# SyncE's order in an attention and expert kernel: where the load of the inverse sums and the load of the transposed activations stand in the queue

## The chip, the cores and the metric

The kernel runs on one core of one Trainium2 chip. The metric is the device time of one execution in microseconds (us), the median of several. The engines are TensorE (PE; its weight loads are shown as PEld), VectorE (DVE), ScalarE (ACT), GpSimd (POOL) and SyncE (SP), which issues nearly all DMAs here. Each engine works through its own instructions strictly in the order of the program, and waits at semaphores.

## The reference, cut to what matters

The input has 8 samples of 512 tokens and 256 channels. Each is normalised (layernorm without weights); then

```python
x = x + attention(xn) + ffn(xn)
# attention: 16 heads of 16 channels; q, k, v and the output each go through a low-rank product
resonance = einsum('bli,hi->blh', x, basis)          # 32 harmonics
q         = einsum('blh,oh->blo', resonance, amp * cos(phase))
out       = softmax(q k^T / 4) v                     # per head, 512 x 512
# ffn: 8 experts (2 per token, weights from a softmax) of width 352, and a shared expert of width 704
```

Before attention the rows of q and k, the low-rank rows and the sums of the softmax are sent through DRAM, since they have to change their place among the partitions.

## The kernel before, in words

**Stages.** The first 366 us or so hold the normalisation, the routing and the routed experts. From about 373 us on the kernel runs the attention of the 8 samples, with the shared expert of each sample woven in between. Only this second stage is touched.

**Slots and steps.** The second stage is a row of slots, called through `slots` on each engine: `slot(b, g)` for sample `b` of 8 and head group `g` of 4 (four heads), after two lead-in slots `(-1, 2)` and `(-1, 3)`. A slot has 8 steps `t`. In each step PE computes one transposed score tile (`score_T`, L1426) into the one PSUM pair `st_pair`, and ACT turns it into exponentials (`exponent`, L1065); `score_T` of step `t` waits for the exponential of step `t - 1`. In the same step PE computes plain scores of the following group (`score`, L1353), of which DVE takes maxima (`maximum`, L1874). The exponentials times the values are PE's L1438. Between these stand pieces of the shared expert (L1402, L1415, L1515), and the small products of the low-rank paths.

**The maxima.** At step 4 PE turns the maxima of the next group (`turn_max`, L1368), at step 5 ACT copies them to `top_T` (`max_rows`, L1024), SyncE sends them to `q_rows` (`load_max`, L632), and the first `score_T` of the next slot waits for that to land.

**The inverse sums.** The sums of the softmax of two groups are gathered into `o_inv` (`move_sums`, L639), and the values into `ao` (`move_values`, L647). In an even slot, step 5, DVE inverts the sums (`invert_sum`, L1924); SyncE stores them to DRAM (`store_inverse`, L652), and in the following odd slot loads them back spread over 128 rows (`load_inverse`, L658) into `o_sum`. It first waits for the store to land. POOL multiplies (`normalise`, L787), and ACT copies the product (`ao_high`, L1077). In ACT's program `ao_high` stands at step 4 of the odd slots, behind that step's exponential, ahead of `max_rows` and of the exponential of step 5. In POOL's program, `hidden` and `hidden_low` of the shared expert and `ao_low` follow `normalise`.

**The low-rank rows.** In slot `(b, 3)`, step 2, PE computes the low-rank product of sample `b + 2` (`low_rank`, L1452) from the transposed activations, which SyncE has loaded (`load_xT`, L588, 1 MB). ACT and DVE split it (L1057 in step 2, L1905 in step 3), and SyncE stores both parts (`store_low_rank`, L607 and L609). In slot `(b, 1)` the like happens for rows of q: PE projects at step 2, ACT splits in step 2 (L1018), DVE in step 3 (L1867), and SyncE stores both parts (`store_qk`, L625 twice and L627).

**SyncE's order before.** An odd slot begins with `load_inverse`, in group 3 followed by `load_x_b` (L597, the residual of the sample, 512 KB), then come the stores of the low-rank rows or of q, then `load_max` and `load_rows` (L551, four loads of 192 KB). In group 2 `load_xT(b + 2)` comes behind `load_rows`. The two buffers of transposed activations, `xT_bs`, are used in turn by `for_rows` (low-rank product) and `for_shared` (shared expert): that of `for_rows(b + 2)` is that of `for_shared(b - 1)`, whose last use lies in slot `(b - 1, 3)`.

The lines on which ACT's order rests are these:

```python
if now:
    exponent(b, g, t)
...
if t == 4 and g % 2 and moved(ppb, ppg // 2):
    ao_high(ppb, ppg // 2)     # waits for p_nm, which normalise on POOL raises
```

Of the kernel before, what the change touches and what calls it, by code (L numbers as in the profile page):

```python
# [33 lines left out]
class Steps:  # L34
# [13 lines left out]
    def wait(self, n=None):  # L48

        self.eng.wait_ge(self.sem, self.value(n))  # L50
# [13 lines left out]
def build_program(nc, x, attn, gate_w, w_gate, w_up, w_down, sw_gate, sw_up, sw_down, out):  # L64
# [45 lines left out]
    def sem(name):  # L110
        return ctx.enter_context(nc.semaphore(name))

    with ctx:
# [218 lines left out]
        b_r, b_v, b_qk, b_s, b_mt, b_st, b_pv, b_gu, b_ha, b_res, b_dn, b_po = (  # L332
            sem(f"b_{n}") for n in ("r", "v", "qk", "s", "mt", "st", "pv", "gu", "ha", "res", "dn", "po"))
# [49 lines left out]
        def for_rows(b):  # L383

            return xT_bs[(b + 1) % 2 if b > 1 else 1]
# [15 lines left out]
        def of(b):  # L401

            return NB - 1 - b

        def there(b):

            return 0 <= b < NB

        def after(b, g, n):

            return (b + (g + n) // NG, (g + n) % NG)
# [14 lines left out]
        def moved(b, p):  # L426

            return there(b) and (b, p) != (LAST, 1)
# [27 lines left out]
        def _(sp):  # L456
# [84 lines left out]
            def load_rows(b, g):  # L541
                for i in range(2):
                    wait(sp, qk_st[i], (b * 2 + g // 2 + 1) * 48)
                if b == 0:
                    sp.wait_ge(minus_st, 16)
                else:
                    wait(sp, b_st, (b - 1) * 32 + g * 8 + 8)
                for which, rows in ((1, k_rows[g]), (0, q_rows[g])):
                    n = 50 if b == 0 and which else 48
                    for i in range(2):  # L550
                        sp.dma_start(rows[64 * i:64 * i + n, :, :].bitcast(F32),  # L551
                                     qk_dram[b % 2, which].rearrange("(j i) r l -> i r j l", i=2)[i][0:n, 2 * g:2 * g + 2, :]).then_inc(qk_in[g], 16)
# [28 lines left out]
            def load_xT(b):  # L581
                if b == 1:
                    for i in range(4):
                        sp.wait_ge(c_st[i], 16 * ((NS + 3 - i) // 4))
                if b == 2:
                    wait(sp, b_r, 2)
                wait(sp, b_gu, (b - 2) * SFT)
                sp.dma_start(for_rows(b)[:, :, :, :].rearrange("p a k l -> p (a k l)").bitcast(F32), xT_dram[of(b)]).then_inc(xT_in, 16)  # L588

            def load_xF(b):  # L590
                wait(sp, b_r, min(b + 2, NB))
                wait(sp, b_gu, (b - 1) * SFT)
                sp.dma_start(for_shared(b)[:, :, :, :].rearrange("p a k l -> p (a k l)").bitcast(F32), xT_dram[of(b)]).then_inc(xF_in, 16)

            def load_x_b(b):
                wait(sp, o_st, b * 32)
                sp.dma_start(o_b[:, :, :], x[of(b)].rearrange("(t p) d -> p t d", p=P)).then_inc(ob_in, 16)  # L597

            def store_out(b, h):
                wait(sp, d_po, b * 2 + h + 1)  # L600
                sp.dma_start(out[of(b), h * 2 * P:(h + 1) * 2 * P, :].rearrange("(t p) d -> p t d", p=P),
                             o_b[:, 2 * h:2 * h + 2, :]).then_inc(o_st, 16)

            def store_low_rank(b):
                wait(sp, r_in, b * 48)
                wait(sp, a_r, b + 1)
                sp.dma_start(r_dram[HI].rearrange("h n l -> n h l"), r_hi[:, :].bitcast(F32)).then_inc(r_st, 16)  # L607
                wait(sp, d_r, b + 1)
                sp.dma_start(r_dram[LO].rearrange("h n l -> n h l"), r_lo[:, :].bitcast(F32)).then_inc(r_st, 16)  # L609

            def load_low_rank(b):
                wait(sp, r_st, (b + 1) * 32)
                wait(sp, b_qk, (b - 1) * 4)
                wait(sp, b_v, (b - 1) * 2)
                for c, part in enumerate((HI, HI, LO)):
                    sp.dma_start(r_rows[b % 2][c * HARM:(c + 1) * HARM, :, :].bitcast(F32), r_dram[part]).then_inc(r_in, 16)

            def store_qk(b, n):
                which, half, i = n % 2, n // 2, n % 2
                if b >= 2:  # L620
                    wait(sp, qk_in[NG - 1], (b - 1) * 64)
                dst = qk_dram[b % 2, which, 8 * half:8 * half + 8, 0:48].rearrange("h (c r) l -> h c r l", c=3)
                wait(sp, a_qk, b * 4 + n + 1)
                for c in ((0, 1), (0, 2))[which]:
                    sp.dma_start(dst[:, c, :, :], qk_hi[i][:, :].bitcast(F32)).then_inc(qk_st[i], 16)  # L625
                wait(sp, d_qk, b * 4 + n + 1)
                sp.dma_start(dst[:, (2, 1)[which], :, :], qk_lo[i][:, :].bitcast(F32)).then_inc(qk_st[i], 16)  # L627

            def load_max(b, g):
                wait(sp, a_mt, b * NG + g + 1)  # L630
                for par in range(2):
                    sp.dma_start(q_rows[g][64 * par + 48:64 * par + 50, :, :].rearrange("a j (t q) -> a j t q", q=P).bitcast(F32),  # L632
                                 top_T[g % 2][16 * par:16 * par + 16, :].bitcast(F32)).then_inc(m_in[g % 2], 16)

            def move_sums(b, g):
                p, h = 2 * b + g // 2, g % 2
                wait(sp, inv_st, p * 16)
                wait(sp, a_ot, b * NG + g + 1)
                sp.dma_start(o_inv[64 * h:64 * h + 64, :], o_T[h][16:128:32, :]).then_inc(sum_in[h], 16)  # L639

            def move_values(b, g):
                p, h = 2 * b + g // 2, g % 2
                wait(sp, p_ao, p)
                wait(sp, a_ot, b * NG + g + 1)
                for j in range(4):
                    o = 64 * h + 16 * j
                    sp.dma_start(ao[o:o + 16, :], o_T[h][32 * j:32 * j + 16, :]).then_inc(ao_in[h], 16)  # L647

            def store_inverse(b, p):
                wait(sp, inv_in, (2 * b + p) * 16)  # L650
                wait(sp, d_inv, 2 * b + p + 1)
                sp.dma_start(inv_dram[p], o_inv[:, :]).then_inc(inv_st, 16)  # L652

            def load_inverse(b, p):
                wait(sp, inv_st, (2 * b + p + 1) * 16)
                wait(sp, p_nm, 2 * b + p)
                heads = inv_dram[p].rearrange("(h o r) l -> h o (r l)", h=8, o=1).to_broadcast([8, 16, L])
                sp.dma_start(o_sum[:, :], heads).then_inc(inv_in, 16)  # L658

            def slot(b, g):  # L660
                (pb, pg), (ppb, ppg), (nb, ng), (rb, rg) = after(b, g, -1), after(b, g, -2), after(b, g, 1), after(b, g, 3)
                if ppg % 2 and moved(ppb, ppg // 2):
                    load_inverse(ppb, ppg // 2)
                if g == 3 and there(b):
                    load_x_b(b)
                if pg % 2 and moved(pb, pg // 2):
                    move_sums(pb, pg)
                    move_values(pb, pg)
                if g == 0 and there(b + 1):
                    store_qk(b + 1, 0)  # L670
                if g == 1 and there(b + 1):
                    store_qk(b + 1, 2)
                if g == 2 and there(b - 1):
                    store_out(b - 1, 0)
                if g == 3 and there(b + 2):
                    store_low_rank(b + 2)
                if there(nb):
                    load_max(nb, ng)
                if there(rb):
                    load_rows(rb, rg)  # L680
                if g == 2 and there(b + 2):
                    load_xT(b + 2)
                if g == 3 and there(b + 2):
                    load_low_rank(b + 2)
                if g == 3 and there(b) and there(b + 1):
                    load_xF(b + 1)
                if pg % 2 == 0 and moved(pb, pg // 2):
                    move_sums(pb, pg)
                    move_values(pb, pg)
                if pg % 2 and moved(pb, pg // 2):  # L690
                    store_inverse(pb, pg // 2)
                if g == 0 and there(b + 1):
                    store_qk(b + 1, 1)
                if g == 1 and there(b + 1):
                    store_qk(b + 1, 3)
                if g == 2 and there(b - 1):
                    store_out(b - 1, 1)

# [1321 lines left out]
```

## Time and profile before

| | |
|---|---|
| median of 3 runs | 979.91 us (979.81 to 980.3) |
| the profiled execution: own time | 981.48 us |
| the profiled execution: span in the profile | 979.7 us |
| PE busy | 878.4 us (90%) |
| DVE busy | 611.4 us (62%) |
| ACT busy | 582.2 us (59%) |
| POOL busy | 400.7 us (41%) |
| mean granted clock of PE | 0.949 of full speed |
| mean DMA traffic | 150 GB/s |

PE is busy for nine tenths of the span, but in the second stage it is tied to the others step by step. The profile's "busy" leaves waiting out; the waits stand in views of their own. In the timeline a row gives the start, the time taken, the engine, the line, the tiles, the shape and the count of instructions merged into it, and in brackets the idle time before it and what ended it. Rows of SPq are issues of DMAs: their time is that of issuing, and not that of the transfer.

### The profile page before, as it was taken

The numbers are of one execution on the slowest core, as the hardware profiler recorded it, in microseconds if no ns is written. First come the engines' busy times: TensorE is split into PE (matmuls) and PEld (weight loads), VectorE is DVE, ScalarE is ACT, GpSimd is POOL, SyncE is SP. The second block draws the span as 40 slices with busy tenths as digits, with TensorE's granted clock in tenths as the row PEclk, the third lists the DMA queues.
The fourth block names the chain that finished last, engine by engine and source line by source line (L and its number), as shares of the span: only waits on it lengthen the run. The fifth ranks groups of instructions, "written<-read, shape, count | busy, mean of one in ns | idle before, by whom it ended". The sixth has DMA issues, their size and how long they took to land.

```text
span 979.7 us, 19365 instructions
## 1 busy us (share of the span) xinstructions
PE 878.4 (90%) x6423; PEld 608.5 (62%) x6424; DVE 611.4 (62%) x923; ACT 582.2 (59%) x932; POOL 400.7 (41%) x384
## 2 busy tenths in 40 slices
PE   4745999999999985788999998999998999999998
PEld 3425999999999982244644644645644645645546
DVE  7777844434434446576786686786786686787642
ACT  5745744444444441477677577677677577677673
POOL 2002622222222203247357356356366356366463
PEclk9865999999999995699999999999999999999999
DMA  9983756222222314356656656667566567564220
GB/s 308 388 249 118 240 143 176 67 75 75 64 75 69 71 57 135 115 132 169 199 144 199 184 149 190 186 155 211 168 154 201 159 154 213 166 161 121 73 83 22
DMA packets 90951, 147.35 MB, mean 150 GB/s; under 512 B 17433, under 2 KB 51745, under 8 KB 88065
## 3 DMA queue, kind: packets, MB, share of 16 engines
q1 hardware_dynamic: 84192, 128.58, 44.5%
q0 software_dynamic: 6480, 17.70, 6.5%
q8 instruction: 43, 0.70, 0.3%
q10 hardware_dynamic: 208, 0.14, 0.1%
q14 instruction: 28, 0.22, 0.1%
HBM read 86.58 MB, written 54.71 MB: 144 GB/s over the span
## 4 chain that ended last, share of the span: by engine, by line
PE 61%; DMA 15%; DVE 14%; SPq 4%; issue 3%; ACT 2%; POOL 1%; ACTq 0%; POOLq 0%; DVEq 0%
PE bank L1438 8%; PE bank L1294 8%; PE s_pair L1276 7%; PE st_pair L1276 7%; DVE top L1874 7%; PE s_pair L1353 6%; PE bank L1402 5%; PE bank L1515 5%; DMA xT_b<-xn_T_split 5%; DMA q_rows<-top_T 4%; PE st_pair L1426 4%; PE bank L1284 2%; PE bank L1259 2%; DMA low_rank_rows<-ro 2%; SPq L632 1%
## 5 line engine op out<-in xcount | busy, mean ns | idle before, releaser
L1874 DVE TENSOR_REDUCE top<-s_pair 128x2 f32<-128x1024 f32 x252 | 308.7, 1225 | 159.9 <-PE s_pair L1353 159.4
L1065 ACT ACTIVATE prob<-st_pair 128x1024 f32<-128x1024 f32 x256 | 262.7, 1026 | 119.1 <-PE st_pair L1426 118.0
L750 POOL DMA_INDIRECT xg<-xn_rows,token_of x71 | 78.9, 1111 | 224.6 <-PE bank L1259 168.9
L1402 PE MATMUL bank<-xT_b,w_sh 64*128 64x512 f32 x960 | 142.5, 401 | 1.0 <-DVE ro L1943 0.2
L1353 PE MATMUL s_pair<-k_rows,q_rows 48*128 48x512 f32 x504 | 121.7, 477 | 20.3 <-DVE top L1874 19.1
L1438 PE MATMUL bank<-prob,v_ones 128*32 128x512 f32 x1024 | 126.4, 612 | 0.0
L1426 PE MATMUL st_pair<-q_rows,k_rows 50*128 50x512 f32 x512 | 110.2, 425 | 17.4 <-DMA q_rows<-top_T 12.9
L796 POOL DMA_INDIRECT y_b<-expert_rows,slot_of x64 | 63.0, 984 | 148.5 <-PE st_pair L1426 141.8
L1402 PEld LDWEIGHTS bank<-xT_b,w_sh 64*128 64x128 f32 x960 | 91.2, 185 | 30.5 <-issue 7.6
L1353 PEld LDWEIGHTS s_pair<-k_rows,q_rows 48*128 48x128 f32 x504 | 49.3, 190 | 77.0 <-DVE top L1874 65.0
L1294 PE MATMUL bank<-w_exp,c_hT 128*128 (+1 forms) x639 | 94.2, 292 | 1.0 <-ACT c_y L985 1.0
L1294 PEld LDWEIGHTS bank<-w_exp,c_hT 128*128 128x128 f32 (+1 forms) x639 | 81.1, 190 | 1.4 <-issue 1.4
L771 POOL TENSOR_TENSOR h_f<-h_f,u_half 128x512 f32<-128x512 f32 x40 | 51.6, 1290 | 72.9 <-DVE h_f L1889 72.9
L1276 PE MATMUL s_pair<-w_exp,xg_T 128*128 x432 | 80.3, 335 | 0.0
L1276 PE MATMUL st_pair<-w_exp,xg_T 128*128 x420 | 76.5, 330 | 0.0
L1426 PEld LDWEIGHTS st_pair<-q_rows,k_rows 50*128 50x128 f32 x512 | 49.7, 189 | 42.4 <-DMA q_rows<-top_T 16.4
L1515 PEld LDWEIGHTS bank<-w_sh,h_T 64*128 64x128 f32 x952 | 66.0, 186 | 8.1 <-issue 2.9
L1276 PEld LDWEIGHTS s_pair<-w_exp,xg_T 128*128 128x128 f32 x432 | 70.5, 192 | 0.3
L1515 PE MATMUL bank<-w_sh,h_T 64*128 64x256 f32 x952 | 70.0, 282 | 0.1
L980 ACT ACTIVATE c_hT<-bank 128x384 fp32r<-128x384 f32 x71 | 34.9, 491 | 55.6 <-PE bank L1284 55.6
L1276 PEld LDWEIGHTS st_pair<-w_exp,xg_T 128*128 128x128 f32 x420 | 66.9, 188 | 0.0
L1438 PEld LDWEIGHTS bank<-prob,v_ones 128*32 128x32 f32 x1024 | 27.1, 110 | 60.2 <-issue 56.6
(234 smaller groups left out, 1201.5 us busy)
## 6 DMA issues: line engine op xcount, KB each, us to landing
xT_b<-xn_T_split SPq DMA_DIRECT2D x14, 1024.0 KB, 7.5
qk_rows<-qk_hi SPq DMA_DIRECT2D x56, 256.0 KB
q_rows<-qk_rows SPq DMA_DIRECT2D x64, 192.0 KB
k_rows<-qk_rows SPq DMA_DIRECT2D x56, 192.0 KB
expert_rows<-c_y SPq DMA_DIRECT2D x71, 128.0 KB, 1.7
xn_T_split<-x_T SPq DMA_DIRECT2D x8, 1024.0 KB, 6.4
qk_rows<-qk_lo SPq DMA_DIRECT2D x28, 256.0 KB
x_all<-in_L_attn_x_dram SPq DMA_DIRECT2D x8, 512.0 KB, 8.3
```

The lines of the kernel that those rows point to most:

```text
L750: pool.indirect_dma_start(xg[s % 4][:, :], None, xn_dram, bass.IndirectOffsetOnAxis(token_of[:, s:s + 1], 0)).then_inc(c_x[s % 4], 16)
L771: pool.tensor_tensor(h, h, u_half[:, :], ALU.mult).then_inc(p_hf, 1)
L796: pool.indirect_dma_start(y_b[:, t, k, :], None, y_dram, bass.IndirectOffsetOnAxis(slot_of[:, k, of(b) * TPB + t:of(b) * TPB + t + 1], 0)) ...
L1065: act.activation(prob[n % 3][:, 2 * jp:2 * jp + 2, :].rearrange("p j l -> p (j l)"), st_pair[:, :], ACT.Exp, scale=HD ** -0.5).then_inc(a_ ...
L1276: ins = pe.matmul(gu_bank[i % 2][n][:, 0:F], xg_T[i % 2][:, a * KT + k, :], w, start=(m == 0 and k == 0), stop=(m == 2 and k == KT - 1))
L1294: ins = pe.matmul(y_bank[:, 0:D], c_hT[i % 2][0:n, a, k, :], w, start=(m == 0 and k == 0), stop=(m == 2 and k == FT - 1))
L1353: ins = pe.matmul(score_pair(b, g, v)[:, i * 512:(i + 1) * 512], q_rows[g][r:r + 48, jp, qt * P:(qt + 1) * P], k_rows[g][r:r + 48, jp, :], ...
L1402: ins = pe.matmul((g_bank, u_bank)[up][:, :], w_sh[rows, a, o:o + P], for_shared(b)[rows, c, k, :], start=(n == 0 and i == 0), stop=(n == ...
L1426: ins = pe.matmul(st_pair[:, i * 512:(i + 1) * 512], k_rows[g][r:r + QK_ROWS, jp, kt * P:(kt + 1) * P], q_rows[g][r:r + QK_ROWS, jp, :], s ...
L1438: ins = pe.matmul(ot_bank[32 * j:32 * j + 32, :], v_ones[:, kt, 4 * g + j, :], prob[(b * 16 + g * 4 + kt) % 3][:, j, :], start=(kt == 0), ...
L1515: ins = pe.matmul((g_bank, u_bank)[to][:, 0:D], h_T[rows, a, f, t * P:(t + 1) * P], w_sh[rows, c, S_GU + f * D:S_GU + (f + 1) * D], start= ...
L1874: dve.tensor_reduce(top[g % 2][:, :, jp, qt], score_pair(b, g, v)[:, :].rearrange("p (i k) -> p i k", i=2), AX_X, ALU.max).then_inc(d_max, 1)
```

## The change

Three things are moved in SyncE's program. `load_inverse` and `load_x_b` go behind `store_qk(b + 1, 0 or 2)`, `store_out` and `store_low_rank`, directly ahead of `load_max`. `load_xT(b + 2)` goes from the middle of slot `(b, 2)` to the end of slot `(b, 1)`, except for the one in the lead-in slot `(-1, 2)`, which stays. `load_xT(b)` waits in addition until the low-rank products of all samples ahead of `b` are done (`b_r >= b`).

```diff
@@ load_xT(b)
                 wait(sp, b_gu, (b - 2) * SFT)
+                wait(sp, b_r, b)
                 sp.dma_start(for_rows(b)[...], xT_dram[of(b)]).then_inc(xT_in, 16)
@@ slot(b, g)
-                if ppg % 2 and moved(ppb, ppg // 2):
-                    load_inverse(ppb, ppg // 2)
-                if g == 3 and there(b):
-                    load_x_b(b)
                 if pg % 2 and moved(pb, pg // 2):
                     move_sums(pb, pg)
                     move_values(pb, pg)
...
                 if g == 3 and there(b + 2):
                     store_low_rank(b + 2)
+                if ppg % 2 and moved(ppb, ppg // 2):
+                    load_inverse(ppb, ppg // 2)
+                if g == 3 and there(b):
+                    load_x_b(b)
                 if there(nb):
                     load_max(nb, ng)
                 if there(rb):
                     load_rows(rb, rg)
-                if g == 2 and there(b + 2):
+                if (b, g) == (-1, 2):
                     load_xT(b + 2)
...
                 if g == 1 and there(b + 1):
                     store_qk(b + 1, 3)
+                if g == 1 and there(b + 2):
+                    load_xT(b + 2)
```

## Rows read from the trace of the kernel before

**Rows 1.** The page, chain that ended last, shares by line.

```profile
PE bank L1438 8%; PE bank L1294 8%; PE s_pair L1276 7%; PE st_pair L1276 7%; DVE top L1874 7%; PE s_pair L1353 6%; PE bank L1402 5%; PE bank L1515 5%; DMA xT_b<-xn_T_split 5%; DMA q_rows<-top_T 4%; PE st_pair L1426 4%; PE bank L1284 2%; PE bank L1259 2%; DMA low_rank_rows<-ro 2%; SPq L632 1%
```

**Rows 2.** Waits of PE and PEld from 440 us on: total, times, longest.

```profile
PE st_pair L1426 <- DMA q_rows<-top_T: 10.6, 8, 2.2
...
PE bank L1452 <- DMA xT_b<-xn_T_split: 3.1, 4, 1.4
...
PEld bank L1452 <- DMA xT_b<-xn_T_split: 6.0, 6, 1.8
```

**Rows 3.** Timeline of SyncE in and ahead of a slot of group 3.

```profile
514.93 0.43 SPq L588 DMA_DIRECT2D xT_b<-xn_T_split  x1
...
522.80 0.65 SPq L658 DMA_DIRECT2D o_sum<-inverse_rows  x1
523.49 0.46 SPq L597 DMA_DIRECT2D o_b<-in_L_attn_x_dram  x1
...
527.09 0.70 SPq L609 DMA_DIRECT2D low_rank_rows<-ro  x1
```

**Rows 4.** Timeline of POOL, ACT and PE in the same slot.

```profile
526.92 1.28 POOL L787 TENSOR_TENSOR ao<-ao,o_sum 128x512 f32<-128x512 f32 x1 [1.30 <-DMA o_sum<-inverse_rows]
...
528.24 0.63 ACT L1077 ACTIVATE ao_T<-ao 128x512 fp32r<-128x512 f32 x1
...
528.98 0.27 ACT L1024 ACTIVATE top_T<-bank 32x128 fp32r<-32x128 f32 x1
...
531.04 0.40 PE L1426 MATMUL st_pair<-q_rows,k_rows 50*128 50x512 f32 x2
...
533.10 1.33 PE L1402 MATMUL bank<-xT_b,w_sh 64*128 64x512 f32 x10
535.57 0.50 PE L1426 MATMUL st_pair<-q_rows,k_rows 50*128 50x512 f32 x2 [1.13 <-DMA q_rows<-top_T]
```

**Rows 5.** Timeline of SyncE, POOL, ACT and PE in a slot of group 1.

```profile
558.34 0.63 SPq L658 DMA_DIRECT2D o_sum<-inverse_rows  x1
...
564.17 0.56 SPq L627 DMA_DIRECT2D qk_rows<-qk_lo  x1
...
563.93 1.29 POOL L787 TENSOR_TENSOR ao<-ao,o_sum 128x512 f32<-128x512 f32 x1 [2.35 <-DMA o_sum<-inverse_rows]
...
565.25 0.63 ACT L1077 ACTIVATE ao_T<-ao 128x512 fp32r<-128x512 f32 x1
...
566.73 1.03 ACT L1065 ACTIVATE prob<-st_pair 128x1024 f32<-128x1024 f32 x1 [0.41 <-PE st_pair L1426]
...
568.54 0.40 PE L1426 MATMUL st_pair<-q_rows,k_rows 50*128 50x512 f32 x2
...
570.03 0.50 PE L1353 MATMUL s_pair<-k_rows,q_rows 48*128 48x512 f32 x2 [0.66 <-DVE top L1874]
```

**Rows 6.** Timeline of the last slot of group 1 that stores rows of q.

```profile
854.80 0.57 SPq L627 DMA_DIRECT2D qk_rows<-qk_lo  x1
...
854.84 0.64 ACT L1077 ACTIVATE ao_T<-ao 128x512 fp32r<-128x512 f32 x1
```

**Rows 7.** Timeline around group 1's end: sums sent, then inverted; POOL's addition.

```profile
575.71 1.26 SPq L639 DMA_DIRECT2D o_inv<-o_T  x1
...
585.24 0.34 DVE L1924 RECIPROCAL o_inv<-o_inv 128x32 f32<-128x32 f32 x1
...
532.60 2.39 POOL L809 TENSOR_TENSOR o_b<-o_b,y_b 128x1024 f32<-128x1024 f32 x1
```

**Rows 8.** Windows: busy time by engine, granted clock of PE, DMA share, GB/s.

```profile
440.00:979.00 539.00, 510.40 (x4080) 293.40 (x4076) 371.83 (x445) 366.55 (x491) 288.05 (x263) 1.00 0.56 157
54.00:58.00 4.00, 0.61 (x2) 0.13 (x2) 3.77 (x8) 2.02 (x1) 0.00 (x0) 0.54 0.51 105
522.00:524.00 2.00, 1.65 (x8) 0.89 (x6) 0.92 (x1) 1.01 (x1) 2.00 (x3) 1.00 0.10 29
```

**Rows 9.** Timeline of PE, the longest idle time ahead of the routing.

```profile
55.53 0.40 PE L1239 MATMUL s_pair<-hot_b,from_here 128*128 128x256 bf16 x1 [4.87 <-DVE hot_b L1764]
```

## The prediction

> **What bounds the kernel now.** I read the chain of waits first [rows 1]: in the attention stage the end is set by PE's own work with short pieces of DVE between, and by DMAs that come late: the transposed activations (5% of the span) and the maxima (4%). That share counts the whole flight of a DMA. What PE really loses stands in the list of waits [rows 2]: 10.6 us in 8 waits for the maxima at the head of a slot, and for the transposed activations 3.1 us on PE and 6.0 us on its weight loads, over six samples. The two overlap, so the move of that load can give 6.0 us at most. In this stage PE is busy for 510.40 of 539.00 us at a granted clock of 1.00 [rows 8]; it has no reserve that could take in a new wait.
>
> Then I read the timeline of SyncE beside those of POOL and ACT, since the change moves the load of the inverse sums, and somebody waits for it. In the slot of group 3 the load is issued at 522.80 [rows 3], `normalise` starts at 526.92 having waited 1.30 us for it, and `ao_high` starts at 528.24, at once behind it [rows 4]. In the slot of group 1 the times are 558.34, 563.93 (after a wait of 2.35 us) and 565.25 [rows 5]. So in both kinds of slot POOL already waits for this load, and ACT takes the product as soon as it is there. What the reader is to see: this load has no slack left. Behind `ao_high` on ACT stand `top_T` and the exponential of step 5, for which PE's `score_T` of step 6 waits.
>
> **Part 1: the load goes behind the stores.** SyncE waits in order. The store of the second low-rank part is issued when DVE has made it, in step 3: at 527.09, for 0.70 us [rows 3]. The load now follows at 527.8 instead of 522.80, 5.0 us later. In group 1 it follows the store of q at 564.17 plus 0.56, so at 564.75 instead of 558.34, 6.4 us later [rows 5]. Both new issues come at about the time at which its product was used (528.24 and 565.25).
>
> How long the load takes: 4.12 us from issue to POOL's start in the one case, 5.59 in the other [rows 3 to 5]. The 4.12 were with a drained queue (29 GB/s in 522 to 524 us [rows 8]). Now the stores stand just ahead of it, small in group 3 (192 KB each), 256 KB three times in group 1. I take 4.2 and 4.6 us, nearer to the drained case, since one store at most is still under way; 4.1 and 5.6 are the bounds.
>
> Group 3: 527.8 + 4.2 = 532.0; `normalise` 1.28; `ao_high` starts at 533.3, 5.1 us later than before. Then `ao_high` 0.63, `top_T` 0.27, the exponential 1.03 [rows 4, 5]: 535.2, where `score_T` of step 6 was at 531.04. With a tenth or so of overlap PE loses 4.1 us in one idle stretch. It does not end there: the first `score_T` of the next slot waits for the maxima, 6.6 us from `top_T` at 528.98 to 535.57, of which 1.13 us were idle [rows 4]. `top_T` is 5.1 us later, so by that rule the next slot starts 5.1 us later. If the maxima land faster, PE's own work decides: 4.1 less the 1.13 that are no longer waited, 3.0 us. I take 4.8, nearer to the upper end, because nothing else in that flight changes. Only where sample `b + 2` exists has the load a store ahead of it: `b` from 0 to 5, six slots, 6 x 4.8 = 29 us.
>
> Group 1: 564.75 + 4.6 + 1.29 + 0.63 + 0.27 + 1.03 = 572.6, less 0.2 of overlap 572.4, against 568.54: 3.9 us. Of these 0.66 are taken in, since PE waited that long for a maximum right behind [rows 5], which DVE now makes meanwhile: 3.2 us. These slots exist for `b` from 1 to 6. In four of the six the store of q ends not 0.5 us ahead of the old `ao_high` but behind it, as in the last (855.37 against 854.84 [rows 6]); part of that lateness ACT already had, so I count 0.7 us more: 2 x 3.2 + 4 x 3.9 = 22 us.
>
> Queued behind the delayed instructions: on POOL `hidden`, `ao_low` and `hidden_low`, three of them, the first of which ACT's copy of the shared expert's rows needs after the exponential of step 5. They run while ACT works off `top_T` and the exponential, so they add nothing. On SyncE `load_max` stands behind the load, but it has to wait for `top_T` anyway, and that comes well after the issue.
>
> **Part 2: the residual's load moved with it.** 512 KB, also issued some 5 us later in group 3. POOL's addition of it starts at 532.60 [rows 7], but POOL itself is now 5 us late, and `normalise` and three more stand ahead of it. Nothing, as long as part 1 holds; without that cover one or two us a sample.
>
> **Part 3: the transposed activations a group ahead.** Issued at the end of group 1's slot, about 575.7 where it stands [rows 7], instead of behind `load_rows` in the next one (the like of 514.93, used at 522.47 [rows 3]). It has most of a slot more to land. That saves between 3.1 and 6.0 us in all [rows 2]; I take 4. The low-rank rows get no longer behind 512 KB of residual, perhaps another 1 us. What the 1 MB is now ahead of: the sums' second move (575.71) and the four moves of values. DVE inverts at 585.24 [rows 7], 9.5 us later; with the 7.5 us that the 1 MB needed from 514.93 to 522.47 that just fits, so 0, at most 1 us a sample. The new wait for `b_r` is for products finished over a slot earlier: 0.
>
> **Part 4: PE's clock.** Each of the twelve slots gets one idle stretch of 3 to 5 us. The longest in this stage was 2.2 us [rows 2], with a clock of 1.00 throughout; in the first stage an idle time of 4.87 us [rows 9] was followed by a clock of 0.54 over 54 to 58 us [rows 8], which mixes the 1.2 and the 2.4 GHz levels. The new stretches lie between. None falling would be 0; all falling for 4 us each, with half of that lost, 24 us. I take 5, nearer to the 2.2 us that changed nothing, as most stretches lie below 4.87.
>
> **Sum.** 29 + 22 - 4 - 1 + 5 = 51 us. The profiled execution (981.48 us, its span 979.7) would become 1032.5; that run is 1.6 us above the median of 979.91, on which I put the same sum: 1031 us. Low bound: even slots 3.0, odd ones 2.7 and 3.4, savings 7, no clock: 18 + 19 - 7 = 30, 1010. High: the loads at 5.6 us, 6 x 6.2 + 22 + 6, savings 3, clock 18: 80, 1060.
>
> **Where a page and the rows differ.** In a drained queue this 256 KB load took 4.12 us until POOL ran. The Trainium skill, page DMA: Bandwidth & Descriptors, section on the anatomy of one DMA, puts a DMA at about 2.0 us fixed plus its bytes at 436 GB/s, an estimate of 2.6 us here (it was fitted on GpSimd's path). With that the sum would be 24 us lower, 1007; the trace does not agree in any of the slots read.
>
> **Rivals.**
>
> A. The load is faster than before, because what slowed it was the traffic of 1 MB and of the row loads, now elsewhere. If it took 2.5 us, the twelve slots would each lose some 1.7 to 2 us less: about 1009. The 4.12 us in the drained queue speak against it [rows 3, 4, 8]. 12%.
>
> B. The clock falls in nearly every stretch. Price 20 us or more above part 4: 1050 to 1065. For it: the fall around the 4.87 us; against: none at 2.2. The skill's page TensorE: Matmul & The Clock Gate, section on the clock gate, says that PE drops to its half rate when it idles long enough and comes back by sustained work, which would speak for B. 10%.
>
> C. Faster: the moved load of the activations removes the wait ahead of the low-rank product, up to 6.0 us, and the stores of the low-rank rows, no longer behind 768 KB, make the low-rank rows early, while ACT is not held: 973. The point from which it decides is the time between the store's end and the product's use. It needs `normalise` done by 528.6 in group 3, that is within 0.8 us of the load's issue, when it alone takes 1.28. Nearly excluded: 2%.
>
> D. The order changes nothing, since SyncE stood at the load until the inverse had been stored, and reached the stores late already: 976 to 981. But 4.3 us lie between the load's issue and that of the last store in group 3 (522.80 and 527.09), 5.8 us in group 1. 2%.
>
> My forecast, 1010 to 1050, keeps 74%. About 0.2% is what a measurement of this kernel can tell from no change. Slower by more than that takes in A, B and the forecast: 0.96; faster 0.02, same 0.02. The range 1005 to 1056 leaves out part of A and of B.
>
> **What would show it.** In the profile after: a new wait of ACT at L1077 for POOL L787 of 3 to 5 us, some twelve times; POOL's wait at L787 for the inverse sums grown from 1.3 to 2.4 us to 6 or more; a new wait of PE at L1426 for ACT's exponential, about 45 us in twelve; the wait at L1452 gone; windows with a clock under 1.00 in the attention stage if part 4 is real. I am wrong if the load is issued after the stores and POOL still starts within 2 us of the old time, or if PE's waits for the exponential stay near nothing.

## The result, and the profile after

The changed kernel takes 1080.22 us (median of 4, 1078.17 to 1085.28) against 980.11 us before (four runs; the 979.91 us above are the median of the first three): a ratio of 1.1000, 95% interval 1.0959 to 1.1041. It is slower by 100 us. The direction is the one forecast, the size is twice the forecast 51 us, and outside the range.

The profiled execution has a span of 1083.5 us (its own time is 1085.28 us, the slowest of the four), so the traces differ by 103.8 us, a little more than the medians (979.7 us before). Lines of the code behind the change stand one to three further down: L658 is now L659, L609 is L610, L787 is L790, L1077 is L1080, L1426 is L1429.

First the page of the changed kernel: busy time, the granted clock in 40 slices, and the chain that ended last.

```profile
PE 914.3 (84%) x6423; PEld 630.5 (58%) x6424; DVE 608.5 (56%) x923; ACT 579.9 (54%) x932; POOL 401.8 (37%) x384
...
PEclk9955999999999757989989888898898988989999
...
DMA o_sum<-inverse_rows 9%; PE bank L1441 8%; PE bank L1405 8%; PE bank L1297 7%; PE s_pair L1356 7%; PE st_pair L1429 6%; PE s_pair L1279 6%; PE st_pair L1279 6%; PE bank L1518 6%; DVE top L1877 4%; PE bank L1287 2%; PE bank L1551 2%; PE bank L1262 2%; ACT prob L1068 2%; POOL ao L790 1%
```

Against [rows 1] the activations and the maxima have gone from the leading shares of the chain, and the load of the inverse sums, which did not stand in it, leads it with 9%. PE's busy time went up from 878.4 to 914.3 us although it runs the same products: 35.9 of the 103.8 us are products that took longer, the other 67.9 us are idle time. From the middle on the clock's digits are 8 about as often as 9, where they were 9 throughout in the kernel before. In the stage from 440 us on, PE's granted clock is 0.90 on average and its products take 545.99 us, against 1.00 and 510.40 us [rows 8].

The list of waits of the changed kernel from 440 us on (total, times, longest) shows the chain of who waited for whom, POOL for the load, ACT for POOL, PE for ACT, and what has gone from PE:

```profile
POOL ao L790 <- DMA o_sum<-inverse_rows: 125.9, 12, 11.1
...
ACT ao_T L1080 <- POOL ao L790: 106.4, 13, 10.3
...
PE st_pair L1429 <- ACT prob L1068: 89.2, 13, 9.1
...
PE s_pair L1356 <- DVE top L1877: 2.1, 5, 1.1
```

Twelve waits of PE for ACT, as predicted, but of 5.6 to 9.1 us and not of some 4 (the thirteenth is 0.4 us). The waits of [rows 2] for the maxima and the activations do not occur any more, and PE's waits for DVE fell from 7.9 to 2.1 us: the long idle stretches took them in.

The timeline of the changed kernel in a slot of group 3, the counterpart of [rows 3, 4], in the order of the chain:

```profile
546.03 0.70 SPq L610 DMA_DIRECT2D low_rank_rows<-ro  x1
546.84 0.65 SPq L659 DMA_DIRECT2D o_sum<-inverse_rows  x1
547.55 0.45 SPq L598 DMA_DIRECT2D o_b<-in_L_attn_x_dram  x1
...
556.16 1.26 POOL L790 TENSOR_TENSOR ao<-ao,o_sum 128x512 f32<-128x512 f32 x1 [11.14 <-DMA o_sum<-inverse_rows]
...
557.45 0.63 ACT L1080 ACTIVATE ao_T<-ao 128x512 fp32r<-128x512 f32 x1 [10.28 <-POOL ao L790]
...
558.14 1.00 ACT L1068 ACTIVATE prob<-st_pair 128x1024 f32<-128x1024 f32 x1
...
559.19 0.80 PE L1429 MATMUL st_pair<-q_rows,k_rows 50*128 50x512 f32 x2 [9.06 <-ACT prob L1068]
```

Every link is where the prediction had it. One number differs: from the issue of the load at 546.84 to POOL's start at 556.16 pass 9.32 us, and 4.2 had been taken. Read in the same way, all six slots of group 3 have 9.1 to 9.3 us. The last row also shows the clock: two products of `score_T` take 0.80 us together where they took 0.40 to 0.50 [rows 4].

In group 1, the counterpart of [rows 5]:

```profile
591.98 0.57 SPq L628 DMA_DIRECT2D qk_rows<-qk_lo  x1
592.65 0.63 SPq L659 DMA_DIRECT2D o_sum<-inverse_rows  x1
...
599.62 1.26 POOL L790 TENSOR_TENSOR ao<-ao,o_sum 128x512 f32<-128x512 f32 x1 [10.24 <-DMA o_sum<-inverse_rows]
...
602.65 0.80 PE L1429 MATMUL st_pair<-q_rows,k_rows 50*128 50x512 f32 x2 [6.15 <-ACT prob L1068]
```

Here the load took 6.97 us (6.4 to 7.0 over the six slots), against the 4.6 taken. In the six slots of group 1 of the kernel before, read in the same way, it had taken 5.4 to 7.4 us already.

What went on in the DMA queue while POOL waited stands in the windows of the changed kernel (length, busy time of PE, PEld, DVE, ACT, POOL, granted clock, DMA share, GB/s):

```profile
546.00:548.00 2.00, 2.00 (x19) 0.55 (x13) 1.73 (x3) 1.17 (x2) 0.00 (x0) 1.00 0.18 47
548.00:550.00 2.00, 2.00 (x16) 1.24 (x14) 1.23 (x1) 0.00 (x0) 0.00 (x0) 1.00 0.69 201
550.00:552.00 2.00, 0.13 (x2) 0.00 (x0) 1.23 (x1) 0.00 (x0) 0.00 (x0) 1.00 0.69 209
552.00:554.00 2.00, 0.00 (x0) 0.00 (x0) 0.00 (x0) 0.00 (x0) 0.00 (x0) 1.00 0.18 63
554.00:556.00 2.00, 0.00 (x0) 0.00 (x0) 0.00 (x0) 0.00 (x0) 0.00 (x0) 0.53 0.12 45
```

In the first window the stores of the low-rank rows are in flight, in the fourth what is left after the bulk of both loads. Both times the 16 engines are busy at 0.18: three of sixteen are 0.19. The trace also records each packet, the pieces in which a DMA moves its bytes, and these say the same: from 546.0 to 547.5 us 3.0 packets are under way at a time, never more than 4, and from 552 to 554 us 3.1, never more than 5. The load had to wait, in a queue that was nearly empty by GB/s, and that is the thing the experiments had to explain. The fifth window shows the second surprise: PE's clock falls in the middle of the wait and is half when work comes back.

### The profile page after: what moved, and what is told of

Read it like the earlier page. It is cut to its first block, busy times and chain, and to the rows that moved or that the text cites. A ratio compares the mean times of both kernels' runs of the same rounds, so it can differ in the third digit from the quotient of the medians.

```text
span 1083.5 us, 19371 instructions
## 1 busy us (share of the span) xinstructions
PE 914.3 (84%) x6423; PEld 630.5 (58%) x6424; DVE 608.5 (56%) x923; ACT 579.9 (54%) x932; POOL 401.8 (37%) x384
## 4 chain that ended last, share of the span: by engine, by line
PE 68%; DMA 12%; DVE 9%; ACT 4%; issue 3%; SPq 2%; POOL 2%; ACTq 0%; POOLq 0%; DVEq 0%
DMA o_sum<-inverse_rows 9%; PE bank L1441 8%; PE bank L1405 8%; PE bank L1297 7%; PE s_pair L1356 7%; PE st_pair L1429 6%; PE s_pair L1279 6%; PE st_pair L1279 6%; PE bank L1518 6%; DVE top L1877 4%; PE bank L1287 2%; PE bank L1551 2%; PE bank L1262 2%; ACT prob L1068 2%; POOL ao L790 1%
## 5 line engine op out<-in xcount | busy, mean ns | idle before, releaser
L1429 PE MATMUL st_pair<-q_rows,k_rows 50*128 50x512 f32 x512 | 120.4, 465 | 95.7 <-ACT prob L1068 92.9
L753 POOL DMA_INDIRECT xg<-xn_rows,token_of x71 | 81.1, 1142 | 222.4 <-PE bank L1262 167.3
L1405 PE MATMUL bank<-xT_b,w_sh 64*128 64x512 f32 x960 | 151.0, 421 | 1.0 <-DVE ro L1946 0.4
L1356 PE MATMUL s_pair<-k_rows,q_rows 48*128 48x512 f32 x504 | 126.0, 494 | 14.0 <-DVE top L1877 12.7
L1441 PE MATMUL bank<-prob,v_ones 128*32 128x512 f32 x1024 | 130.0, 627 | 0.0
L1429 PEld LDWEIGHTS st_pair<-q_rows,k_rows 50*128 50x128 f32 x512 | 53.8, 205 | 125.5 <-ACT prob L1068 107.7
L1405 PEld LDWEIGHTS bank<-xT_b,w_sh 64*128 64x128 f32 x960 | 96.9, 198 | 31.8 <-issue 6.8
L1356 PEld LDWEIGHTS s_pair<-k_rows,q_rows 48*128 48x128 f32 x504 | 52.2, 202 | 71.5 <-DVE top L1877 53.8
L1080 ACT ACTIVATE ao_T<-ao 128x512 fp32r<-128x512 f32 x15 | 9.5, 631 | 106.4 <-POOL ao L790 106.4
L790 POOL TENSOR_TENSOR ao<-ao,o_sum 128x512 f32<-128x512 f32 x15 | 19.0, 1267 | 126.0 <-DMA o_sum<-inverse_rows 125.9
```

The lines of the kernel that those rows point to most:

```text
L753: pool.indirect_dma_start(xg[s % 4][:, :], None, xn_dram, bass.IndirectOffsetOnAxis(token_of[:, s:s + 1], 0)).then_inc(c_x[s % 4], 16)
L1356: ins = pe.matmul(score_pair(b, g, v)[:, i * 512:(i + 1) * 512], q_rows[g][r:r + 48, jp, qt * P:(qt + 1) * P], k_rows[g][r:r + 48, jp, :], ...
L1405: ins = pe.matmul((g_bank, u_bank)[up][:, :], w_sh[rows, a, o:o + P], for_shared(b)[rows, c, k, :], start=(n == 0 and i == 0), stop=(n == ...
L1429: ins = pe.matmul(st_pair[:, i * 512:(i + 1) * 512], k_rows[g][r:r + QK_ROWS, jp, kt * P:(kt + 1) * P], q_rows[g][r:r + QK_ROWS, jp, :], s ...
L1441: ins = pe.matmul(ot_bank[32 * j:32 * j + 32, :], v_ones[:, kt, 4 * g + j, :], prob[(b * 16 + g * 4 + kt) % 3][:, j, :], start=(kt == 0), ...
```

## The experiments

**Theory 1** after the result: the loss comes from the load of the inverse sums alone. It is late twice, since it is issued late and then stands in the DMA queue behind stores; the idle time that follows costs PE its clock too. **Rivals**: the activations' load has a share; the residual's 512 KB stretch the flight; the flight is long at that time of the slot whatever stands ahead; the clock costs nothing. Each ratio below is against the kernel before, run on the same chip as the experiment.

**The change in its two halves.** `e1` moves only the load of the activations:

```diff
--- changed kernel
+++ e1_activations_only
@@ slot(b, g) of SyncE
+                if ppg % 2 and moved(ppb, ppg // 2):
+                    load_inverse(ppb, ppg // 2)
+                if g == 3 and there(b):
+                    load_x_b(b)
                 if pg % 2 and moved(pb, pg // 2):
...
                     store_low_rank(b + 2)
-                if ppg % 2 and moved(ppb, ppg // 2):
-                    load_inverse(ppb, ppg // 2)
-                if g == 3 and there(b):
-                    load_x_b(b)
```

> Only the load of the transposed activations moves; the loads of the inverse sums and of the residual stay where they were. Theory 1 (the loss comes from the load of the inverse sums alone): the wait ahead of the low-rank product goes, 973 to 978 us. Rival (1 MB ahead of the sums' second move delays these, and that is part of the loss): 985 us or more.

Measured: 979.0 us (10 runs) against 982.45 us of the kernel before on the same chip, ratio 0.9968 (0.9946 to 0.9990): a gain of 3 us. The time lies 1 us above what was expected. PE's wait for the activations is gone, but its wait for the maxima stays:

```profile
PE st_pair L1429 <- DMA q_rows<-top_T: 7.7, 6, 1.9
```

`e2` moves only the other two loads:

```diff
--- changed kernel
+++ e2_inverse_only
-                if (b, g) == (-1, 2):
+                if g == 2 and there(b + 2):
                     load_xT(b + 2)
...
-                if g == 1 and there(b + 2):
-                    load_xT(b + 2)
```

> Only the loads of the inverse sums and of the residual move. Theory 1: nearly all of the loss, 1080 to 1088 us, a few us more than the changed kernel, since the activations come late again. Rival (the activations' load has its share in the loss): 1060 us or less.

Measured: 1084.21 us, ratio 1.1058 (1.0996 to 1.1119). The whole loss belongs to this half. The 4 us more than the change lie within the intervals. With `e1`, which has no loss, the load of the activations is innocent.

**The two kinds of slot.** `e6` keeps the load late in group 3 alone, `e7` in group 1 alone:

```diff
--- changed kernel
+++ e6_late_in_group_3
+                if g == 1 and ppg % 2 and moved(ppb, ppg // 2):
+                    load_inverse(ppb, ppg // 2)
                 if pg % 2 and moved(pb, pg // 2):
...
-                if ppg % 2 and moved(ppb, ppg // 2):
+                if g == 3 and ppg % 2 and moved(ppb, ppg // 2):
                     load_inverse(ppb, ppg // 2)
--- changed kernel
+++ e7_late_in_group_1
+                if g == 3 and ppg % 2 and moved(ppb, ppg // 2):
+                    load_inverse(ppb, ppg // 2)
+                if g == 3 and there(b):
+                    load_x_b(b)
                 if pg % 2 and moved(pb, pg // 2):
...
-                if ppg % 2 and moved(ppb, ppg // 2):
+                if g == 1 and ppg % 2 and moved(ppb, ppg // 2):
                     load_inverse(ppb, ppg // 2)
-                if g == 3 and there(b):
-                    load_x_b(b)
```

> The changed kernel with the load of the inverse sums back at the head of the slot in group 1; it is late in group 3 alone, six slots. Theory 1 (each kind of slot pays for itself: 9.0 us of idle time and a low clock in group 3, 5.8 in group 1): some 60 of the 100 us remain, 1035 to 1045 us. Rival (the slots work on each other: a sample that is late in one group is late in the next anyway, so that most of the loss stays): 1060 us or more.

> The changed kernel with the load of the inverse sums, and that of the residual, back at the head of the slot in group 3; the first is late in group 1 alone. Theory 1 (the two groups' losses add up): 100 us less the 57 that group 3 alone kept, so 1018 to 1026 us, with a flight of 6.2 to 7 us and idle stretches of 5.5 to 6.2. Rival (they overlap): 1035 us or more.

Measured: 1036.87 us, ratio 1.0554 (1.0497 to 1.0611), and 1023.04 us, ratio 1.0467 (1.0424 to 1.0510). In parts of the time before these are 5.5% and 4.7%, together 10.2%, and the change has 10.0%. The slots pay each for itself: some 9 us for each of the six in group 3, some 7.5 us for each in group 1. The windows of the stage, of `e6` and then of `e7`, show what of this is slower products:

```profile
440.00:1037.00 597.00, 528.12 (x4083) 306.25 (x4082) 372.26 (x445) 366.20 (x492) 288.55 (x263) 0.93 0.52 140
```

```profile
440.00:1022.00 582.00, 527.36 (x4080) 301.13 (x4076) 375.58 (x445) 366.11 (x491) 287.80 (x263) 0.96 0.52 144
```

PE's products take 17.7 and 17.0 us more than the 510.40 of the kernel before, each time for six idle stretches: some 3 us a stretch.

**Late by issue, or late in the queue.** `e3` lets SyncE wait for both parts as in the change, and then issues the load first and the stores behind it. So the issue is as late as in the change, and only what stands ahead in the queue differs.

```diff
--- changed kernel
+++ e3_load_ahead_of_stores
                 if g == 1 and there(b + 1):
+                    wait(sp, a_qk, (b + 1) * 4 + 3)
+                    wait(sp, d_qk, (b + 1) * 4 + 3)
+                if g == 3 and there(b + 2):
+                    wait(sp, a_r, b + 3)
+                    wait(sp, d_r, b + 3)
+                if ppg % 2 and moved(ppb, ppg // 2):
+                    load_inverse(ppb, ppg // 2)
+                if g == 1 and there(b + 1):
                     store_qk(b + 1, 2)
...
                     store_low_rank(b + 2)
-                if ppg % 2 and moved(ppb, ppg // 2):
-                    load_inverse(ppb, ppg // 2)
```

> The changed kernel, but SyncE, having waited for both parts in step 3, issues the load of the inverse sums first and the stores behind it. The issue comes about as late as in the change. Theory 1 (the load is late twice: it is issued late, and then it stands behind the stores in the DMA queue, 9.3 us of flight in group 3 and 6.6 in group 1 against 4.1): the flight falls to 4 to 5 us, PE's idle stretches from 9.0 and 5.8 to about 4, and the time to 1020 to 1045 us. Rival (at this time of the slot the load is slow whatever stands ahead of it): flight 6 us or more, 1070 us or more.

Measured: 1053.13 us, ratio 1.0700 (1.0646 to 1.0753). The flight did what theory 1 said; the time did not come down as far. SyncE, POOL and PE of this kernel, in a slot of group 3:

```profile
544.22 0.65 SPq L659 DMA_DIRECT2D o_sum<-inverse_rows  x1
...
548.09 1.26 POOL L796 TENSOR_TENSOR ao<-ao,o_sum 128x512 f32<-128x512 f32 x1 [4.92 <-DMA o_sum<-inverse_rows]
...
551.12 0.50 PE L1435 MATMUL st_pair<-q_rows,k_rows 50*128 50x512 f32 x2 [2.83 <-ACT prob L1074]
551.46 0.39 PE L1411 MATMUL bank<-xT_b,w_sh 64*128 64x512 f32 x2
...
552.37 0.79 PE L1411 MATMUL bank<-xT_b,w_sh 64*128 64x512 f32 x2
...
558.60 0.50 PE L1435 MATMUL st_pair<-q_rows,k_rows 50*128 50x512 f32 x2 [2.54 <-DMA q_rows<-top_T]
```

The flight is 3.87 us here, 3.8 to 4.3 over all twelve slots, in both groups. The load is not slow at that time of the slot; the stores ahead of it made 2.5 and 5.2 us of its flight. PE's idle stretches at this place fell to 2.4 to 3.1 us. The time lies 8 us above the expectation, and the rows show two things that it had left out. The clock falls even after 2.83 us: the same pair of products takes 0.39 us at 551.46 and 0.79 at 552.37. It does so in all twelve slots, behind stretches of 2.40 to 3.11 us. And the maxima, sent behind the stores, now come late in the next slot (2.54 us, the last row; 13.7 us over six slots).

**The residual.** `e4` puts the 512 KB load back to the head of the slot:

```diff
--- changed kernel
+++ e4_residual_back
+                if g == 3 and there(b):
+                    load_x_b(b)
                 if pg % 2 and moved(pb, pg // 2):
...
-                if g == 3 and there(b):
-                    load_x_b(b)
```

> The changed kernel with the load of the residual (512 KB) back at the head of the slot of group 3. Theory 1 (the store ahead sets the flight): the flight in group 3 stays near 9 us, 1073 to 1085 us. Rival (the 512 KB that follow the load share its DMA engines and stretch it): the flight in group 3 falls to 5 to 6 us, PE's idle stretches there to 5, and the time to about 1050 us.

Measured: 1080.98 us, ratio 1.1002 (1.0955 to 1.1049), with a flight of 8.9 to 9.0 us in group 3. The residual is worth 0.4 us of flight and nothing in the time. That rival has fallen.

**Three engines of sixteen.** The buffer of the low-rank rows in DRAM is laid out as 32 x 3 x 512, and the store writes it through a view of 3 x 32 x 512. `e8` lays it out as 3 x 32 x 512, so that a store is 96 rows in one run, and the load takes the view instead. (Of the stage itself the second store and the load are shown; the first store, the two stores ahead of the stage and the load of the first sample's values are altered in the same way.)

```diff
--- changed kernel
+++ e8_low_rank_rows_spread
-    r_dram = nc.dram_tensor("low_rank_rows", (2, 32, 3, L), F32).ap()
+    r_dram = nc.dram_tensor("low_rank_rows", (2, 3, 32, L), F32).ap()
...
-                sp.dma_start(r_dram[LO].rearrange("h n l -> n h l"), r_lo[:, :].bitcast(F32)).then_inc(r_st, 16)
+                sp.dma_start(r_dram[LO].rearrange("n h l -> (n h) l"), r_lo[:, :].bitcast(F32)).then_inc(r_st, 16)
...
-                    sp.dma_start(r_rows[b % 2][c * HARM:(c + 1) * HARM, :, :].bitcast(F32), r_dram[part]).then_inc(r_in, 16)
+                    sp.dma_start(r_rows[b % 2][c * HARM:(c + 1) * HARM, :, :].bitcast(F32), r_dram[part].rearrange("n h l -> h n l")).then_inc(r_in, 16)
```

> The changed kernel with the buffer of the low-rank rows in DRAM laid out as the rows lie in SBUF, so that a store is one run of 96 rows and not three of 32. Theory 1 (the two stores ahead of the load use 3 of the 16 DMA engines, the share of 0.18 in the windows, and the load has to wait for just these): the share goes up, the flight in group 3 falls from 9.3 to 4 to 6 us, PE's idle stretches there from 9.0 to about 5, those of group 1 stay, and the time is 1040 to 1058 us. Rival (a store of 192 KB is slow however it is spread, since it goes to DRAM): 1073 us or more.

Measured: 1044.26 us, ratio 1.0641 (1.0581 to 1.0700), 36 us less than the change, with the same bytes in the same order of issue. (The load of these rows, which now goes through the view, comes behind all of this in the queue.) SyncE, POOL and the window behind the issue:

```profile
533.84 0.32 SPq L610 DMA_DIRECT2D low_rank_rows<-ro  x1
534.25 0.65 SPq L659 DMA_DIRECT2D o_sum<-inverse_rows  x1
...
538.46 1.26 POOL L790 TENSOR_TENSOR ao<-ao,o_sum 128x512 f32<-128x512 f32 x1 [5.63 <-DMA o_sum<-inverse_rows]
```

```profile
534.00:536.00 2.00, 2.00 (x21) 0.69 (x15) 1.53 (x2) 0.97 (x2) 0.00 (x0) 1.00 0.43 112
```

The flight in group 3 fell to 4.21 us (3.8 to 5.3 over the six), the share rose from 0.18 to 0.43, and even the issue of the store takes 0.32 us on SyncE and not 0.70. In group 1, where nothing was altered, the flight stayed at 6.2 to 7.0 us. While the second store runs (534.8 to 535.2 us) 15.6 packets are under way at a time, where the change had 3.0. So the stores ahead were slow because they used few engines. That the load shares just these engines is inferred from the packets, the share and the flight; no row names an engine. The Trainium skill, page DMA: Bandwidth & Descriptors, section "Why a DMA increments its semaphore by 16 and not by 1", gives the rule behind it: a DMA is spread over the largest number up to 16 that divides the slowest dimension (other than 1) of both sides, and those issued as here are given the lowest-numbered engines. By that rule 3 x 32 x 512 against 96 rows gives 3, and 96 rows against 96 rows gives 16; the 3.0 and 15.6 packets agree, while which engines they are no run here shows.

**The clock by itself.** `e5` gives PE products that nobody reads, ahead of `score_T` of step 6, where it would stand idle:

```diff
--- changed kernel
+++ e5_dummy_products
@@ slot(b, g) of PE
+                    if (g, t) == (1, 6) and 1 <= b < LAST:
+                        wait(pe, a_uh, lows(b, 0))
+                        for n in range(20):
+                            pe.matmul(u_bank[:, :], basis_T[...], for_shared(b)[:, HI, 0, :], start=True, stop=True)
+                    if (g, t) == (3, 6) and 0 <= b < LAST - 1:
+                        for n in range(8):
+                            pe.matmul(m_bank[64:128, :], basis_T[...].bitcast(F32), for_shared(b)[:, HI, 0, :].bitcast(F32), start=True, stop=True)
                     if now:
                         score_T(b, g, t)
```

> The changed kernel, with products whose results nobody reads put on PE ahead of score_T of step 6 in the twelve slots (20 in group 1, 8 slower ones in group 3), where PE would stand idle; nothing else is moved and the output stays the same. Theory 1 (besides the idle time itself, PE loses time because its clock falls to half in each stretch and stays there when work comes back): the clock stays at 1.00 and the time falls to 1055 to 1070 us. Rival (the clock costs nothing, the other engines set the pace after the stretch): 1076 us or more.

Measured: 1065.96 us, ratio 1.0857 (1.0798 to 1.0917). Flights and the lateness of ACT are those of the change; only PE's idle time is filled. The slot of group 3 and the windows of the whole stage, of this kernel and then of the changed one:

```profile
543.74 7.08 PE L1615 MATMUL bank<-xT_b,basis_T 128*64 128x512 f32 x16
552.86 0.50 PE L1429 MATMUL st_pair<-q_rows,k_rows 50*128 50x512 f32 x2 [2.04 <-ACT prob L1068]
```

```profile
440.00:1063.00 623.00, 591.86 (x4284) 334.67 (x4280) 367.69 (x443) 363.07 (x490) 287.35 (x262) 0.98 0.50 134
```

```profile
440.00:1083.00 643.00, 545.99 (x4101) 314.10 (x4099) 370.85 (x447) 366.07 (x494) 287.69 (x263) 0.90 0.49 131
```

The mean clock of the stage rises from 0.90 to 0.98, `score_T` behind the wait takes 0.50 us and not 0.80, and the time falls by 14 us (20 between the two profiled executions). That is a lower bound of what the clock costs, since it did not stay at 1.00 throughout, as theory 1 had it. An upper bound is what all products together take longer in the change, 35.6 us in this stage.

**Better than both.** `e9` is `e1` with the layout of `e8`, `e10` the kernel before with the layout alone:

```diff
--- kernel before
+++ e10_spread_only          (e9: the same on top of e1)
-    r_dram = nc.dram_tensor("low_rank_rows", (2, 32, 3, L), F32).ap()
+    r_dram = nc.dram_tensor("low_rank_rows", (2, 3, 32, L), F32).ap()
...
```

> The loads of the inverse sums and of the residual where they were before, the activations a group ahead, and the low-rank rows laid out as in the run before. Theory 1: the maxima sent behind the stores in group 3 land sooner, the wait of PE at the head of the next slot goes, and the time is 966 to 974 us. Rival (that flight has its length from its own small pieces): 975 to 981 us.

> The kernel before with the low-rank rows laid out as in the two runs above and nothing else: the load of the activations stays in group 2, the load of the inverse sums at the head of the slot. Theory 1 (the two gains are apart: some 3 us from the activations, the rest from the layout): 964 to 969 us, and the wait of PE for the activations is still there. Rival (each needs the other, since without the layout the activations' gain is eaten by the next wait, and the other way round): 970 us or more.

Measured: `e9` 961.91 us, ratio 0.9791 (0.9749 to 0.9833); `e10` 963.43 us, ratio 0.9839 (0.9811 to 0.9867). Both beat both kernels, and both lie below what was expected, `e9` by 4 us and `e10` by 0.6. The waits of PE from 440 us on, first of `e9`, then of `e10`:

```profile
PE s_pair L1356 <- DVE top L1877: 9.6, 24, 1.1
PE st_pair L1561 <- ACT o_T L1075: 1.0, 1, 1.0
```

```profile
PE s_pair L1353 <- DVE top L1874: 7.2, 19, 1.1
PE bank L1452 <- DMA xT_b<-xn_T_split: 2.6, 4, 1.2
```

The 10.6 us of waiting for the maxima [rows 2] are gone in both. Six of those eight waits stood at the head of a slot of group 0, for maxima that had been sent behind the low-rank stores; the other two stood at the head of a slot of group 1, and why they went too is not shown. The activations' wait stays in `e10` and goes in `e9`. The gains roughly add up, 0.3% from the activations and 1.6% from the layout against 2.1% for both, within the intervals.

## Why the prediction was wrong

**What bounds, and who waits: right.** That the load had no slack, that ACT takes its product in step 4 ahead of `top_T` and of the next exponential, that PE then stands in front of `score_T` of step 6, in twelve slots: all as forecast, link by link. `e2` shows that all of the loss is here.

**Part 1, the load's flight: the first step that failed.** It said "I take 4.2 and 4.6 us, nearer to the drained case, since one store at most is still under way". It measured 9.1 to 9.3 and 6.4 to 7.0. Nearness was judged by how much of the queue was filled, and the right question was how long the thing directly ahead takes. The trace of before had the answer: its chain of waits has the store of the second low-rank part in flight for more than 7 us, in two of the slots,

```profile
671.79 7.63 DMA low_rank_rows<-ro
...
817.52 7.48 DMA low_rank_rows<-ro
```

and its windows right behind that store have 0.19 of the DMA engines at 59 GB/s:

```profile
528.00:530.00 2.00, 2.00 (x19) 1.04 (x13) 1.37 (x3) 1.46 (x4) 1.33 (x2) 1.00 0.19 59
```

The window that the prediction read, 522 to 524 us, lies ahead of the stores and was a drained queue indeed; this one, in which the moved load would run, was three engines at work. In group 1 the 4.6 us lay below all six flights of the kernel before, 5.4 to 7.4 us, and the upper bound of 5.6 below three of them. The excess of flight is 5.1 us in six slots and some 2 in the other six, 43 us. `e3` takes it away in both groups and `e8` in group 3, in two independent ways, and they leave flights of 3.8 to 5.3 us, about what had been taken.

**The next slot's maxima.** The 4.8 us for a slot of group 3 had the rule that `top_T`'s lateness is passed on in full. In the changed kernel the next slot does not wait for the maxima at all, since SyncE sends them long after the stores are through. So the loss per slot is set by the idle stretch, 9.06 us less what it takes in, and the 6.6 us from `top_T` to the next slot was no constant: with the stores spread, in `e9` and `e10`, that wait is gone.

**Part 2, the residual at nothing: right** (`e4`, 1080.98 us). **Part 3, 4 us for the activations and 0 for what stands behind them: right in size** (`e1`, 3 us, with an interval of 1 to 5).

**Part 4, the clock: the second step that failed, a term of the right kind and too small.** Taken were 5 us; measured were 14 us at least (`e5`) and 35.6 us of longer products at most. The choice "nearer to the 2.2 us that changed nothing" was wrong: the clock fell behind all twelve stretches of 5.6 to 9.1 us, and in `e3`, where the flights were as short as the prediction had them, behind all twelve of 2.40 to 3.11. So this term would have failed with the right flights too.

**How the 51 us became 103.8 in the traces.** PE's twelve stretches come to 88.8 us, where the sum had 6 x 4.1 and 6 x 3.9 = 48; these 41 us more are about the excess of flight. But part of them was taken in: PE's idle time rose by 67.9 us in all, since its waits for the maxima, for DVE and for the activations went or shrank, and the sum had 46 for it (29 + 22 - 4 - 1). So idle time was short by 22 us, and the products, 35.9 us longer against the 5 taken, by 31. This says where PE's time went; what each cause is worth by itself is known only as `e3`, `e5` and `e8` give it, 27, 14 and 36 us, and these overlap.

**Where a page and the rows differed.** The 2.6 us from the page's fixed time and rate were no better: no flight of this load was under 3.8 us in any run. (The 24 us that this was to take off the sum do not come out of it either: 1.6 us in six slots and 2.0 in six are 22.) What did bear on it was how the transfer ahead is spread over the DMA engines. Rival A fell with the flights. B was right that the clock falls in every stretch, and its price, 20 us or more above the 5, lies between the two bounds above; the time left its range because of the flights. C and D fell.

## What to carry to other kernels

Before a transfer is put behind another in one queue, look at that other's own flight and at how many DMA engines it uses, not at the queue's GB/s: here two stores of 192 KB on three engines held the load behind them up by 5 us. The cure was a layout in DRAM that lets the store run as one block of rows, and it was worth more (16 us, `e10`) than the order of the issues (3 us, `e1`). When an engine in the middle of a lockstep takes a product at a fixed place in its program, its supply may be moved only by the slack that the trace shows, which here was none. And idle stretches of PE are to be priced with the slower products behind them, here some 3 us each.

## What the runs showed of the hardware

PE's granted clock fell from 2.4 to 1.2 GHz after shorter idle time than expected: from 440 us on never in the kernel before, whose longest idle stretch was 2.18 us, but in `e3` behind all twelve stretches of 2.40 to 3.11 us, in the slot shown only once work had come back (0.39 us for a pair of products at 551.46, 0.79 us at 552.37). Idle time alone does not decide: in `e5` the six slots of group 3 have 1.92 to 2.08 us of idle time behind the unread products, and the clock fell behind three of them and stayed at 2.4 GHz behind the other three.

The issue of a DMA costs SyncE itself by its form as well: 0.70 us for the store in three parts, 0.32 us for the same bytes in one.

Left open: what the layout of the stores of q, three of 256 KB, costs in group 1, where they hold the load up by some 2.5 us. Packets under way at a time are 8.2 on average from 592 to 597 us, while these stores and the load run, so about half of the 16 engines was in use. By the rule for the spread of a DMA that the Trainium skill gives, page DMA: Bandwidth & Descriptors, section "Why a DMA increments its semaphore by 16 and not by 1", these stores, 8 x 16 x 512 against 128 rows, use 8 engines, and the packets agree. No run changed their layout.
